# Preparing the last attention two one-hot rounds ahead, and its first unit's scores put before two rotations

## The reference, cut to what matters

```
x  = x + tanh(g) * attention(layernorm(x), ctx)
q  = (query @ Wq)  -> 32 heads of 128;  k, v -> 8 heads of 128, each used by 4 query heads
cos = cos_t[position_ids];  sin = sin_t[position_ids]
q  = q * cos + rotate_half(q) * sin;    k = k * cos + rotate_half(k) * sin
scores = q k^T / sqrt(128);  masked scores = -1e9;  attn = softmax(scores)
out = (attn @ v) @ Wo
```

## Time and profile before

| | us |
|---|---|
| median of 3 runs | 2186.48 (2184.53 to 2188.93) |
| the profiled execution | 2186.74 |
| its span | 2184.9 |
| preparation of the last attention, in the span | 1142.2 to 1206.9 |
| first matmul of the last attention | 1207.76 |

### The profile page before, as it was taken

How to read it: one execution, slowest core, us unless ns; L and a number is a source line. 1 busy time by engine, 2 the same in 40 slices (tenths; PEclk the granted TensorE clock), 3 DMA queues, 4 the chain that set the end, 5 groups by cost and what they waited for, 6 DMA issues and landing times. The chain is left out here.

```text
span 2184.9 us, 37129 instructions
## 1 busy us (share of the span) xinstructions
PE 1860.1 (85%) x14832; PEld 1034.9 (47%) x14832; DVE 1671.9 (77%) x2989; ACT 557.4 (26%) x1290; POOL 599.5 (27%) x717
## 2 busy tenths in 40 slices
PE   4388788887788888988855899999999999999876
PEld 3344455444554355533632355555555555555432
DVE  3379766798658966699644788888888888888875
ACT  3121223222342123222224122222222222222221
POOL 0220114102140023300224443434343434343210
PEclk7689978999899987999967999999999999999987
DMA  7436501473033720436013211111111111110100
GB/s 231 154 103 191 152 2 39 132 204 111 1 103 115 204 63 1 137 116 174 1 43 127 78 49 49 49 49 49 49 50 51 52 51 51 49 30 20 40 25 35
DMA packets 134266, 176.47 MB, mean 81 GB/s; under 512 B 46416, under 2 KB 73200, under 8 KB 133968
## 3 DMA queue, kind: packets, MB, share of 16 engines
q1 hardware_dynamic: 134096, 174.10, 26.5%
HBM read 131.98 MB, written 42.08 MB: 80 GB/s over the span
## 5 line engine op out<-in xcount | busy, mean ns | idle before, releaser
L1156 POOL TENSOR_TENSOR early_vare<-early_mv,w_eps 128x1 f32<-128x1 f32 x96 | 30.1, 313 | 779.0 <-DVE early_mv L1222 764.9
L379 PE MATMUL la_ps<-w_xTh,w_wqh 128*128 128x512 bf16 x512 | 198.4, 388 | 15.4 <-DVE la_rot L2271 10.3
L2210 POOL TENSOR_TENSOR la_q<-la_straight,la_rot 128x512 f32<-128x512 f32 x128 | 163.1, 1274 | 164.7 <-DVE la_rot L2271 164.7
L379 PE MATMUL la_ps<-w_woh,la_oTh 128*128 128x512 bf16 x512 | 199.2, 389 | 0.0
L380 PE MATMUL la_ps<-w_wol,la_oTh 128*128 128x512 bf16 x512 | 198.8, 388 | 0.0
L750 PE MATMUL early_ps<-early_products,w_heads 128*32 128x512 f32 x1024 | 146.0, 698 | 61.0 <-DVE early_products L1373 34.9
L381 PE MATMUL la_ps<-w_woh,la_oTl 128*128 128x512 bf16 x512 | 197.8, 386 | 0.0
L380 PE MATMUL la_ps<-w_xTl,w_wqh 128*128 128x512 bf16 x512 | 196.7, 384 | 0.0
L381 PE MATMUL la_ps<-w_xTh,w_wql 128*128 128x512 bf16 x512 | 196.6, 384 | 0.0
L2223 POOL TENSOR_TENSOR la_p<-la_s,la_rec 128x256 f32<-128x256 f32 x128 | 89.6, 700 | 322.4 <-DVE la_rec L2292 322.4
L2161 ACT ACTIVATE la_oTh<-la_ps 128x256 bf16<-128x256 f32 x256 | 84.2, 381 | 303.1 <-PE la_ps L2073 303.1
(11 more groups left out here) (345 smaller groups left out, 4535.2 us busy)
## 6 DMA issues: line engine op xcount, KB each, us to landing
early_vR<-scr_v SPq DMA_DIRECT2D x128, 257.0 KB, 5.2
early_wkv<-wkv SPq DMA_DIRECT2D x32, 512.0 KB, 4.6
la_v<-v SPq DMA_DIRECT2D x64, 256.0 KB, 3.9
k<-early_ctxt SPq DMA_DIRECT2D x32, 256.0 KB, 3.7
v<-early_ctxt SPq DMA_DIRECT2D x64, 128.0 KB, 3.1
scr_p<-early_weights SPq DMA_DIRECT2D x16, 512.0 KB, 3.1
early_pR<-scr_p SPq DMA_DIRECT2D x32, 256.0 KB, 3.4
w_raw_q<-in_Wq SPq DMA_DIRECT2D x8, 1024.0 KB, 6.9
```

The lines of the kernel that those rows point to most:

```text
L379: pe.matmul(out, lh[c], rh[c], start=(first and c == 0), stop=False)
L2210: rope_sum.send(pool.tensor_tensor(dst, straight[:, slot, :], rot[:, slot, :], ALU.add))
```

## The change

The one-hot rows get two buffers, used in turn, and `hot(t)` waits only for `rope(t-2)`. DVE writes `hot(0)` and `hot(1)` before its first statistics and takes `statistics(0)`, `statistics(1)`, `hot(2)`, `low(0)`, `statistics(2)`, `hot(3)` and so on. On SP the positions and the table are loaded ahead of the first tiles of x. ACT copies the looked-up cos and sin one place earlier: `half_rope(0)` stands before `normalise(1)`, and each further one before the next `normalise` or, for the last, before the split of Wo. In the attention the last entry of `FIRST` is projected after the first unit's scores, and DVE's softmax and POOL's division of that unit stand before the last two rotations.

```diff
-        one_hot = sb("one_hot", [P, C, QUAD * P])
+        one_hot = sb("one_hot", [P, 2, C, QUAD * P])
...
-            load_x(0)
             pos_loaded.send(sp.dma_start(pos[:, :], io["pos3"].partition_broadcast(P)))
             table_loaded.send(sp.dma_start(table[:, :, :], io["rope"].rearrange("(c p) n -> p c n", p=P)))
+            load_x(0)
             load_x(1)
...
-                    last = pe.matmul(banks.bank("rope", t), table[:, c, :], one_hot[:, c, :],
+                    last = pe.matmul(banks.bank("rope", t), table[:, c, :], one_hot[:, t % 2, c, :],
...
             normalise(0)
+            half_rope(0)
             normalise(1)
             high(0)
-            half_rope(0)
+            half_rope(1)
             normalise(2)
             act.wait_ge(q_loaded.sem, 16)
             high_q(0)
             high_q(1)
             high(1)
-            half_rope(1)
+            half_rope(2)
             normalise(3)
             high_q(2)
             high_q(3)
             high(2)
-            half_rope(2)
+            half_rope(3)
             act.wait_ge(o_loaded.sem, 16)
             for h in range(GROUP):
                 high_o(h)
             high(3)
-            half_rope(3)
...
             def hot(t):
-                if t >= 1:
-                    banks.wait_filled(dve, 0, "rope", t - 1)
+                if t >= 2:
+                    banks.wait_filled(dve, 0, "rope", t - 2)
...
-            statistics(0)
             dve.wait_ge(pos_loaded.sem, 16)
             dve.wait_ge(row_ready.sem, 1)
             hot(0)
+            hot(1)
+            statistics(0)
             statistics(1)
+            hot(2)
             low(0)
             statistics(2)
-            hot(1)
+            hot(3)
             low(1)
             statistics(3)
-            hot(2)
             low(2)
-            hot(3)
...
-            for place, which, step in FIRST:
+            for place, which, step in FIRST[:6]:
                 if which is not None:
                     project_q(0, place, step, which)
             rope_sum.wait(pe, 0, 4)
             scores(0, ("score", "first"), 0, 0)
+            for place, which, step in FIRST[6:]:
+                project_q(0, place, step, which)
...
             for i, (place, which, step) in enumerate(FIRST):
+                if i == 5:
+                    divide(0, 0, 0)
                 add_rotation(0, place, i % 2, rotated(which, step))
-            divide(0, 0, 0)
...
             for i, (place, _, step) in enumerate(FIRST):
+                if i == 5:
+                    softmax(0, Steps(dve, first_step, 2, 0), ("score", "first"), 0, 0, 0)
                 rotate(0, i, i % 2, place, step)
-            softmax(0, Steps(dve, first_step, 2, 0), ("score", "first"), 0, 0, 0)
```

More of the change, by code:

```diff
@@ L1750, in hot @@
             def hot(t):
-                if t >= 1:
-                    banks.wait_filled(dve, 0, "rope", t - 1)
+                if t >= 2:
+                    banks.wait_filled(dve, 0, "rope", t - 2)
                 for c in range(C):
-                    last = dve.tensor_scalar(one_hot[:, c, :], pos[:, tokens(t)], row[:, c:c + 1], None, ALU.is_equal)
+                    last = dve.tensor_scalar(one_hot[:, t % 2, c, :], pos[:, tokens(t)], row[:, c:c + 1], None, ALU.is_equal)
                 hot_ready.send(last)
```

## The result

| | before | changed |
|---|---|---|
| median, 15 runs each | 2186.31 us | 2179.51 us |
| single runs | 2179.1 to 2194.8 | 2171.6 to 2186.9 |
| profiled execution, its span | 2186.74, 2184.9 | 2175.81, 2174.0 |

The ratio is 0.9963 with a 95% interval of 0.9945 to 0.9982. The direction is the forecast one; the size, 8 us by the ratio (6.8 by the medians), lies just past the end of the predicted range (2178.8 is 0.9965 of the 2186.48 it was reckoned from). The forecast itself, 0.9978, lies inside the interval. Runs of a disturbed chip are left out of all comparisons, and the one profile taken in such an execution, that of `short_filled`, isn't read.

The account below looks back on a forecast made before the run. It took the preparation to be bound by a ring over DVE, POOL and ACT ending on POOL, the attention by PE; 2186.74 − 7.3 + 2.3 = 2181.7 us, range 2178.8 to 2184.8 for 8 in 10.

Parts of the forecast that it names:

- The sum: Whole kernel: 2186.74 less 7.3 from the preparation plus 2.3 from the attention's start gives 2181.7 us.
- POOL's two waits: End of the preparation: POOL's waits for ACT's cos and sin, 2.53 and 3.59 us, 6.1 together, go.
- The last offset: Preparation, POOL: the last round's offset comes 1.2 us early, at 1183.1.
- The start: Preparation's first link: positions and two one-hot rounds first make the first statistics 3.4 us late; positions possibly 2.4 later.
- the positions land late: Rival, preparation's start: positions land 2.4 us late, shifting every link, 2184.1; chance 0.25 shared with two slow clock stretches.
- The end on POOL: Copies moved on ACT are ready before POOL needs them; POOL still closes the stage, which ends 7.3 us earlier.
- The attention: Attention's start: reordering leaves PE idle 3.5 us before unit 0's projection and costs 2.3 us, from 0.7 to 4.0.
- DVE's wait: Attention's start: DVE idles about 2 us before the first softmax, from 1225.14 to 1227.3.
- delay of 2.26: Attention: first products with v start at 1237.45 instead of 1235.19, and everything queued behind on PE is delayed.
- the 1.6 that the sum laid to that stretch: Attention, PE: about 1.6 us lost in before's 3.3 us at 1.2 GHz; one such stretch assumed again, so nothing added.
- The cheap gap: Rival, attention's start: PE's clock stays up after the gap, which costs 0.7 us; 2180.1 us, chance 0.17.
- Rope never got into the ring: Rival, preparation: unfinished `rope` holds up ACT's next `normalise` and the round-to-round ring, 6.0 us each twice; 2193.7, chance 0.04.

Follow-up runs that it names:

- short_filled: Changed kernel without its early layers, plus 14 unread matmuls in PE's gap in the attention: 1107.7 us, against 1107.28 without the matmuls.
- short kernels: Kernels before and changed with the early layers left out, each timed twice: medians 1114.88 and 1113.68 us before, 1110.98 and 1107.28 changed.
- prep_only: Changed preparation with the attention of before, against the kernel before: ratio 0.9948 (0.9926 to 0.9970), preparation 56.9 us.
- filled_gap: Changed kernel with 14 unread matmuls in PE's gap in the attention, against the kernel before: ratio 0.9960 (0.9942 to 0.9977).
- copies_late: As prep_only, but ACT's copies of cos and sin where the kernel before has them: one run, 2166.56 us, preparation 56.7 us.
- one_buffer: Kernel before with one one-hot buffer, DVE's one-hot rounds from the second on one place earlier: ratio 0.9960 (0.9931 to 0.9988), preparation 56.1 us.
- control: Kernel before with the one-hot tile twice as large, only its first half used, no order changed: ratio 1.0003 (0.9982 to 1.0025).
- short_before: Kernel before with its early layers left out, x, keys and values taken from inputs, run twice: medians 1114.88 and 1113.68 us.
- x_first: As prep_only, but first tiles of x loaded first and first statistics ahead of all one-hot rows, against before: ratio 0.9966, preparation 55.8 us.
- stats_early: As x_first, with DVE's later statistics ahead of an earlier round's remainders, against before: ratio 0.9915, median 2171.29 us, preparation 47.3 us.
- after_again: The changed kernel timed once more, unchanged, against the kernel before: ratio 0.9982 (0.9964 to 0.9999).

## Why the prediction was right or wrong

- **What failed: the range, and the sizes of two terms.** The sum said −5.0. The short kernels say −3.9 and −6.4, and the landmarks' means (preparation 57.1 in six profiles with the edit, `prep_only` among them but not its variants, 65.1 in seven without; A3 44.5 in seven with the new start, filled_gap not counted, 42.4 in nine without) give −8.0 + 2.1 = −5.9. "What a measurement can tell from no change is about 0.2%" was taken for the error of one comparison, and the range 2178.8 to 2184.8 was built from the mechanisms alone. But single runs of before reach from 2174 to 2198, and two comparisons of one and the same pair gave −8 and −4. The range needed some 4 us on either side for the draw of unchanged layers, on top of the mechanisms. Twelve profiles of whole kernels have the iota between 1129.8 and 1149.7, while the rest behind A3 is 933.2 to 935.6 in all of them. By these landmarks it is that spread that put the first timing past the end; the 15 runs themselves have no landmarks, so it isn't shown for them. The repeat falls in the range.
- **The terms.** POOL's two waits, put at 6.1 from one profile, are 6.1 in two and 7.0 to 7.7 in five of the seven profiles with the old preparation, 7.0 in the mean. The last offset, forecast 1.2 early, came between 0.1 late and 1.6 early, 0.8 in the mean. That makes −7.8 of the −8.0, where −7.3 was forecast. The first profile of the changed kernel is a poor case of both: offset 0.1 late, waits 6.1.
- **The start: right, with its bound.** Positions first cost the first link 3.0 to 4.1 in five profiles, 3.5 of it in prep_only, and 5.0 in the changed kernel's first, where they landed 1.3 later than in prep_only. The rival "the positions land late" thus came about in part.
- **The end on POOL: the size nearly right, the reason wrong.** "Both after their copies, so its two waits go" holds. But the step laid it to the copies' new place on ACT; copies_late and one_buffer show that the place is worth nothing. The waits fell because `rope` no longer stands before `turn_x` on PE when ACT comes for `high(3)`.
- **The attention: the mean right by luck.** The gap (3.4 where no record is missing, 3.5 forecast) and DVE's wait fit. So does the delay of 2.26 at the first products: 28.6 to 28.9 against 26.5 and 26.7 in control and prep_only, whose clock rose as early. That this delay "stays in the time" does not hold: two units on, A3 is 42.6 to 42.9 against 41.5 and 41.8, so 1.1 of it is left. With the old start PE waits for DVE there, 1.29 in copies_late and in both profiles of short_before (PE's timeline of copies_late):

```profile
1219.79 0.38 PE L379 MATMUL la_ps<-w_woh,la_oTh 128*128 128x512 bf16 x1 [1.29 <-DVE la_oTl L2299]
```

  With the new start PE idles only 0.30 there where the clock stays up. The row of 22.50 busy us came behind a slow stretch that had hidden it: all four profiles with the old start whose clock fell lack the wait, all five whose clock stayed up have it. So the 1.6 that the sum laid to that stretch was mostly not lost; by an estimate along the profiles without a fall (A3 of 41.5 at a rise of 2.8, 42.7 at 5.8) it was 0.4 of before's 42.6. And where the clock falls in the new gap, the part costs 3.4 at a like rise (46.0, 45.9 and 46.1 against 42.4 to 42.8) or 2.4 (45.1 against 42.7), not 2.3. A single value was the wrong form: it is 1.1 or 2.4 to 3.4.
- **The rivals.** The cheap gap is the case of three profiles of seven, at 1.1 instead of 0.7. Rope never got into the ring where the positions came first; in x_first and stats_early ACT waited 2.23 and 3.41 for `rope(0)`, and the second `normalise` came 0.4 and 1.4 after its offset was ready. The Trainium skill, "TensorE: Matmul & The Clock Gate", section "What's actually happening", has the low rate as the default, which activity releases. By that rule the sum would have had 1.7 more; the trace agrees in three profiles of seven, where the slow stretch behind the long gap lasted 6.8 us instead of 3.4, and not in the other four.

## What to carry to other kernels

When a stage's engines wait for each other in turn, look for the instruction that stands one place too late in one queue before adding buffers: three lines of order on DVE gave what two buffers and three other reorderings gave, and taking the statistics out of the ring gave twice that. Price an idle gap on the matrix engine with both outcomes of its clock, and compare two profiles of a stage only where the clock rose at a like time in it. And before a gain of 0.2% is forecast or believed, see how far single runs of the same kernel lie apart and in which stage; in a copy of the program that holds only the edited stages they lay 1 to 6 us apart, in the whole 14 to 22.

## What the hardware showed that I had not expected

The unchanged layers differ between executions by up to 20 us of 1140. The granted clock differs with them; in the first 400 us (windows, before and then changed) it is 0.84 and 0.87:

```profile
0.00:400.00 400.00, 292.50 (x2516) 179.54 (x2517) 256.31 (x401) 106.23 (x215) 76.17 (x121) 0.84 0.43 129
```

```profile
0.00:400.00 400.00, 292.70 (x2544) 178.61 (x2552) 264.86 (x417) 109.23 (x221) 79.70 (x129) 0.87 0.43 132
```

Over the twelve whole kernels the two go together: up to the iota, the mean granted clock is 0.88 in the two that reach it first (1129.8 and 1134.9) and 0.87 in the three that reach it last (1149.0 to 1149.7). PE's busy time up to there goes from 893 to 912 us in the twelve, while DVE's stays within 825 to 827. Whether the clock is the cause was not tried.

The same instructions with the same gap of about 3.4 us had PE's clock fall in four executions and stay up in three, and which of the two came went with when the clock had risen at the start of the stage, over 20 us before. In after_again, PE is busy 1.62 of 3.50 around the gap's end and keeps 2.4 GHz:

```profile
1230.50:1234.00 3.50, 1.62 (x8) 0.80 (x9) 3.32 (x6) 0.02 (x1) 2.30 (x2) 1.00 0.00 0
1234.00:1239.50 5.50, 5.03 (x44) 2.76 (x42) 4.95 (x8) 1.44 (x4) 2.25 (x2) 1.00 0.20 45
```

The positions, a megabyte written from an 8 KB source as the first transfer of the stage, landed between 3.4 and 5.9 after the iota in the six profiles above with the changed preparation: the first transfer behind a barrier is not a fixed time.
